# Expanding the split queries of a softmax layer: three transfers of 24 rows for each half

## What is computed

```python
q, k, v = proj(Wq, bq), proj(Wk, bk), proj(Wv, bv)          # 16 heads of 8
scores = einsum('bhqd,bhkd->bhqk', q, k) * scale            # masked (0, 2) or + bias (3)
p = softmax(scores - max(scores))
out = einsum('bhqk,bhkd->bhqd', p, v) @ Wo.T + bo
```

## Time and profile before

| What | us |
|---|---|
| Median of 3 runs | 2870.99 (2866.79 to 2872.88) |
| The profiled execution's own time | 2863.05 |
| Its span in the trace | 2861.2 |
| PE busy in the span | 2431.9 (85%) |
| DVE busy | 1534.3 (54%) |
| ACT busy | 1340.6 (47%) |
| POOL busy | 564.8 (20%) |

### The profile page before, as it was taken

One profiled execution on the slowest core, in us unless ns is written; L12 is line 12 of the kernel. 1 busy time (PEld: TensorE's weight loads), 2 busy tenths in 40 slices (PEclk: granted clock), 3 DMA queues, 4 the chain that ended last, 5 costly groups with the idle time before them and its releaser, 6 DMA issues. The chain is left out here.

```text
span 2861.2 us, 45685 instructions
## 1 busy us (share of the span) xinstructions
PE 2431.9 (85%) x15607; PEld 1470.4 (51%) x15730; DVE 1534.3 (54%) x4364; ACT 1340.6 (47%) x2454; POOL 564.8 (20%) x591
## 2 busy tenths in 40 slices
PE   4688788899994799999996799988886888898887
PEld 2345444588883466666795344444442433444333
DVE  4577667411112366555533566666646776777663
ACT  3355444544443333333134355555551666666665
POOL 1433333000003654553001111111100001111000
PEclk9899999999997799999998699999996999999999
DMA  3222222377773100000264211111102111111011
GB/s 115 75 72 77 77 71 65 105 213 204 207 209 111 29 23 22 23 26 10 80 195 116 71 43 51 51 52 53 57 15 86 46 51 51 51 46 40 33 39 32
DMA packets 132374, 214.08 MB, mean 75 GB/s; under 512 B 22664, under 2 KB 91824, under 8 KB 125232
## 3 DMA queue, kind: packets, MB, share of 16 engines
q1 hardware_dynamic: 119024, 186.88, 22.4%
q0 software_dynamic: 10240, 20.99, 2.6%
q10 hardware_dynamic: 2880, 3.28, 0.4%
HBM read 158.50 MB, written 51.40 MB: 73 GB/s over the span
## 5 line engine op out<-in xcount | busy, mean ns | idle before, releaser
L534 DVE TENSOR_REDUCE arena<-bank 128x1 f32<-128x512 f32 (+4 forms) x1216 | 725.5, 616 | 491.3 <-PE bank L523 258.7
L609 ACT ACTIVATE arena<-bank 128x512 f32<-128x512 f32 x640 | 374.7, 599 | 422.6 <-PE bank L599 349.2
L517 PE MATMUL bank<-arena 125*128 125x512 bf16 (+3 forms) x1536 | 478.5, 348 | 33.5 <-DMA arena<-q_parts 18.4
L587 PE MATMUL bank<-arena 128*128 128x512 bf16 (+3 forms) x1413 | 407.6, 333 | 106.5 <-ACT arena L609 69.7
L609 ACT ACTIVATE arena<-bank,arena 128x512 f32<-128x512 f32 x512 | 337.7, 688 | 213.7 <-PE bank L587 80.9
L587 PEld LDWEIGHTS bank<-arena 128*128 128x128 bf16 x1536 | 139.3, 101 | 413.4 <-ACT arena L609 255.7
L624 PE MATMUL bank<-arena 128*32 128x512 f32 (+3 forms) x3072 | 333.9, 517 | 1.4 <-ACT arena L609 0.8
L938 POOL DMA_INDIRECT back_rows<-sorted_out,back_now x160 | 154.7, 967 | 515.8 <-PE bank L599 231.3
L517 PEld LDWEIGHTS bank<-arena 125*128 125x128 bf16 x1536 | 146.8, 102 | 206.7 <-DVE arena L534 89.0
L1177 ACT ACTIVATE arena<-bank,arena 128x256 f32<-128x256 f32 x320 | 131.9, 471 | 160.0 <-PE bank L1227 160.0
L1022 PE MATMUL bank<-arena 128*128 128x128 f32 x1664 | 202.5, 275 | 0.3 <-ACT arena L1177 0.3
(11 more groups left out here) (250 smaller groups left out, 3558.2 us busy)
## 6 DMA issues: line engine op xcount, KB each, us to landing
arena<-k_parts SPq DMA_DIRECT2D x48, 576.0 KB
arena<-q_parts SPq DMA_DIRECT2D x48, 576.0 KB
arena<-in_L_ffn_w SPq DMA_DIRECT2D x80, 320.0 KB, 3.6
arena<-in_L_ffn_w SPq DMA_DIRECT2D x80, 258.0 KB, 3.1
arena<-sorted_in SPq DMA_DIRECT2D x104, 128.0 KB, 2.5
sorted_out<-arena SPq DMA_DIRECT2D x104, 128.0 KB, 3.5
arena<-in_L_ffn_w SPq DMA_DIRECT2D x24, 512.0 KB, 4.0
k_parts<-arena SPq DMA_DIRECT2D x24, 384.0 KB
```

The source lines that it names most:

```text
L517: ins = pe.matmul(mx[:, k * w:(k + 1) * w], Qx[0:KMAX, h, q * P:(q + 1) * P], Kx[0:KMAX, h, 0:w], start=(k == 0 or not L.causal), stop=not ...
L534: ins = dve.reduce_max(L.mx[:, g % 2, q, heads[0]:heads[-1] + 1], mx[:, 0:w * len(heads) - far].rearrange("p (j k) -> p j k", k=w - far), ...
L587: ins = pe.matmul(st[:, c:c + w], Kx[:, h, kb * P:(kb + 1) * P], Qx[:, h, T - w:T], start=(c == 0), stop=not (L.causal or far), skip_group ...
L609: act.activation(L.probs[:, n % L.PR, 0:w], st[:, 0:w], ACT.Exp, scale=L.scale).then_inc(L.st_free.sem, 1)
```

## The change

Each of the two transfers that fill `Qx` (one for each half of the heads) becomes three, one for each block of 24 rows. They read the same 24 rows of `q_parts` without a repeated dimension. The semaphore of that half counts three completions, and the wait in `pe_max` asks for three. The transfers for `Kx`, the bytes moved and their place in the queue stay: per batch 2 + 6 in place of 2 + 2 transfers.

```diff
-            L.qx = [s(f"q_expanded{i}_", 16, 1) for i in range(HALVES)]
+            L.qx = [s(f"q_expanded{i}_", 16 * NPART, 1) for i in range(HALVES)]
...
-            q_rows = L.qd.rearrange("d i (o h) t -> o (d i) h t", o=1)
+            q_rows = L.qd.rearrange("d i h t -> (d i) h t")
...
-                sp.dma_start(copy_of(L.Qx, b)[0:KROWS, heads, :], q_rows[:, :, heads, :].rearrange(
-                    "o r h t -> o r (h t)").to_broadcast([NPART, NPART * HD, H * T // HALVES])).then_inc(L.qx[half].sem, 16)
+                for j in range(NPART):
+                    sp.dma_start(copy_of(L.Qx, b)[j * NPART * HD:(j + 1) * NPART * HD, heads, :],
+                                 q_rows[:, heads, :]).then_inc(L.qx[half].sem, 16)
...
-                pe.wait_ge(L.qx[half].sem, L.qx[half].at(b, 16))
+                pe.wait_ge(L.qx[half].sem, L.qx[half].at(b, 16 * NPART))
```

## The result

Over 20 runs of each, the changed kernel takes 2884.9 us (2864.8 to 2896.9) and the kernel before 2868.8 (2859.3 to 2876.3): ratio 1.0044, 95% interval 1.0027 to 1.006. The forecast was 2826 us. The profiled execution took 2874.11 us, its span is 2872.3 us against 2861.2, so the two traces hold 11.1 of the 16 us between the medians; the rest lies in executions that weren't profiled.

What follows compares the result with a forecast made beforehand. PE, busy 85% of the span, was taken as the bound, so PE's idle time counts. Gains of 7.5 + 6.5 + 0.3 + 18 + 10 + 3 = 45 us off the 2870.99 us median gave 2826 us, range 2805 to 2857.

Steps and rivals of the forecast that it cites:

- Slower: Rival, chance 0.05: under 160 GB/s, layer 3's max rows stay in line from end to end; 2880 to 2905 us.
- the rate: Expansion transfers: 24 rows spread as `Kx` does go at 209 GB/s, 5.6 us a half, both halves about 12.5 us.
- who holds the row: Layer 3's max row, 6.4 us beside the three-engine tail, would land about 4.6 us after its issue.
- The 3 us for the clock: Layer 3: a shorter stop may spare PE's fall to half clock after the wait; 3 us, between 0 and 8.
- Layer 2's rows: A half is through before the max row is sent, so nearly all 20.0 us of waits go; 18 us less.
- The starts: Starts of layers 0 and 3: `Qx` arrives earlier, 7.5 and 6.5 us less.
- my 5.6 + 2.2: A half's transfer at 209 GB/s plus issue to release when alone: `Qx` 7.8 us after the issue of `Kx`.
- Layer 2's 0.3 us: Start of layer 2: at most 0.3 us less, since its products are in the way.
- Issue: SP's queue: two more issues cost 1.45 us a half, but end no wait of PE; costed at nothing.
- It doesn't spread: Rival, chance 0.06: blocks stay on three engines or run one after the other; +3 us, 2874 us.

Runs made afterwards that it cites:

- e5: Changed kernel, but each half of q is one transfer, 24 rows outermost and three copies inside, parts wrongly paired; ratio 0.9916 to the kernel before.
- e6: Changed kernel, but each block goes to every third partition, parts wrongly paired; ratio 0.9893 to the kernel before.
- e1: Blocks in layers 0 and 2 alone, layer 3 keeps its one transfer; ratio 0.9923 to the kernel before.
- e2: Blocks in layer 3 alone, the old form elsewhere; ratio 1.0085 to the kernel before.
- e4: Kernel before, but layer 3's expansion waits for the third max row of the batch before it, not the second; ratio 0.9939 to the kernel before.
- c4: Kernel before, but in layer 3 the second half of an expansion waits for the third max row; ratio 0.9952 to the kernel before.
- e3: Changed kernel, but layer 3's expansion waits for the third max row of the batch before it, not the second; ratio 0.9842 to the kernel before.
- c3: Changed kernel, but in layer 3 the second half of an expansion waits for the third max row; ratio 0.9802 to the kernel before.
- s1: Changed kernel with a 512-byte transfer behind each block, so that blocks are issued slower; ratio 0.9958 to the kernel before.
- e7: q's parts stored three times in DRAM, each half of q then one plain transfer of 72 rows; ratio 1.0029 to the kernel before.

## Why the prediction was wrong

- **The right mechanism with the wrong sign in layer 3.** That max rows queue with the expansion is what moves this kernel, up and down. The rival *Slower* named what happened, with its place (layer 3's rows in line from end to end) and its condition (under 160 GB/s): its 2880 to 2905 holds the 2884.9. It had a chance of 0.05. Its price was too high in layer 2, which loses nothing, and right in layer 3: 3 to 7 us more in six places, 27 us in all for its 28.
- **The step that failed: the rate.** I took 209 GB/s for a stretch that "holds `Kx` and `Qx` packets together" as what 12 engines give for any transfer. That stretch begins 2 us after the first issue and is mostly `Kx`. The blocks alone had no row before; their rate should have been bounded from below by something else, and the lower bound put into the range. Both halves take 16.8 to 20.1 us for a forecast of 12.5, and no wide form of `Qx` got under 13.9.
- **The second step that failed: who holds the row.** I put layer 3's late row down to the tail on three engines. That is where it was the earlier trace rows, but a wide transfer holds it longer. In e5, which has no tail and 180 GB/s:
```profile
2231.61 0.79 SPq L492 DMA_DIRECT2D arena<-k_parts  x1
...
2238.98 0.72 ACTq L500 DMA_DIRECT2D arena<-arena  x1
...
2247.20 0.61 PE L587 MATMUL bank<-arena 128*128 128x512 bf16 x1 [4.34 <-DMA arena<-arena]
```
  it is in after 8.2 us, for 6.4 with the tail and 11.5 with the blocks. The packets in the traces say why. Alone, the first of a row's 12 packets starts 1.4 us after the issue; here it starts 4.1, 6.4 and 7.5 us after it (before, e5, after). What SP's queue (q1) moved until then, in this order, and below that what both queues moved from there on in before (q10 is ACT's; packets, MB, share of 16 engines):
```profile
q1 hardware_dynamic: 38, 0.29, 19.0%
q1 hardware_dynamic: 162, 1.14, 74.5%
q1 hardware_dynamic: 163, 1.02, 77.4%
...
q1 hardware_dynamic: 14, 0.11, 17.8%
q10 hardware_dynamic: 13, 0.01, 2.1%
```
  That is 77 GB/s on three engines and 179 and 137 on twelve, so a packet of 8 KB takes an engine about 0.32, 0.55 and 0.72 us. The row's first packet is late by 8.5, 9.1 and 8.5 of these: as many go ahead of it on its engine in each form. From there the queues take turns, 13 packets of the row's queue and 14 of SP's in 1.55 us, which costs up to four more for the rest of the row. So a row waits for a number of packets, some 12 in all, and its time is that of a packet: the fewer bytes an engine gets in a microsecond, the later the row. (An estimate; which engine a packet used isn't in the trace.) The step sums say it in time: e5 184.3 and e6 179.0, against 175.6 to 178.4 with the old form. So the 10 us for layer 3's rows weren't to be had at the 180 to 197 GB/s that the best forms reach. The 3 us for the clock went with them: PE stops longer and PEclk is 0.51 for 6 us after.
- **Layer 2's rows: mechanism right.** All its waits are gone, the rows no longer come late, and e1 shows the gain by itself. The two traces differ by 8.6 us there, not 18; over four kernels with each form (before, e2, e4, c4; after, e1, e3, c3) the means are 518.4 and 503.9 us, so the term is 14.5. Part of the scatter is the clock after one of DVE's waits, which both kernels have. Before, with its clock by stretch:
```profile
1851.14 1.12 PE L2006 MATMUL bank<-arena 32*128 32x512 f32 x2 [1.57 <-DVE arena L2044]
...
1853.00:1855.00 2.00, 2.00 (x13) 1.15 (x10) 1.51 (x3) 1.17 (x3) 0.00 (x0) 0.50 0.02 5
1857.00:1859.00 2.00, 2.00 (x22) 1.18 (x14) 1.01 (x2) 0.60 (x1) 0.00 (x0) 1.00 0.48 127
```
and after:
```profile
1975.28 2.07 PE L2007 MATMUL bank<-arena 32*128 32x512 f32 x2 [1.57 <-DVE arena L2045]
...
1975.00:1977.00 2.00, 1.72 (x2) 0.50 (x2) 0.82 (x2) 0.72 (x2) 0.00 (x0) 0.50 0.51 165
1993.00:1995.00 2.00, 2.00 (x13) 0.72 (x15) 1.22 (x2) 0.60 (x1) 0.00 (x0) 0.50 0.74 102
1995.00:1997.00 2.00, 2.00 (x18) 0.76 (x10) 0.69 (x1) 0.75 (x2) 0.00 (x0) 0.93 0.63 107
```
  The same stop of 1.57 us, in different batches of the layer, is followed by 3 to 4 us at 1.2 GHz in the one case and 20 in the other. That the change lengthens it isn't shown: over layer 2's rows the low clock lasts 44 us in before and 58 in after, but 72 in e4 (old form) and 38 in e1 (blocks).
- **The starts: half the size.** 3.8 and 3.5 us for 7.5 and 6.5. Of the 3.4 us that layer 0 missed, the rate is 2: in e5 the first product comes 9.1 us after the first issue (32.8, 41.89), with the blocks 11.2. The other 1.3 are my 5.6 + 2.2, too short even for a fast transfer. Layer 2's 0.3 us can't be told from the scatter.
- **Issue.** The second half's `Kx` is issued 2.24 us after the first one, for 1.6 before, so the two more issues cost 0.6 us in a half and not 1.45, and nothing waits for them. Nothing was right as a price, but slower issue makes these blocks faster (s1).
- **The rule that two transfers to disjoint partitions serialize** (the Trainium skill, page "DMA: Bandwidth & Descriptors", section "Rules for kernel authors"), the ground of the rival *It doesn't spread*, didn't decide here: the blocks did spread, at a share of 0.70 to 0.84.

## What to carry to other kernels

Before a large transfer is spread over more engines, list the small transfers that are sent while it is in flight and who waits for them: on each engine they stand behind packets that now move more slowly, and they gain only if the large one is through before they are sent. If it isn't, order the two: one more entry in a table turned this change from 0.4% slower into 2% faster (each against the old kernel on its own chip). And take a rate from a stretch in which that transfer is alone.

## What the runs showed of the hardware

- The same packets to 24 neighbouring partitions, at the same DMA share of 0.75 to 0.79, move 119 to 139 GB/s, and 188 to 197 when each block is spread over every third of 72 and issued at a slower pace (0.78 us apart for 0.4 to 0.6). A busy share says nothing of bytes.
- Issued 1.1 to 1.2 us apart with a small transfer between them, the neighbouring blocks reach 177 to 185; read from three separate copies at the quick pace, 174 to 194.
- A transfer of 24 rows into neighbouring partitions costs SP 0.366 us to issue, to every third partition 0.704, one of 72 rows 0.727 to 0.764 where its source repeats rows and 0.534 where it doesn't (e7).
- A 12 KB transfer takes 2.2 us alone, up to 5.1 beside one half of blocks and 11.5 beside two, although it is on another queue: by the estimate above 8 to 9 packets of 8 KB go ahead of its first on an engine, then the queues take turns. The Trainium skill, page "DMA: Bandwidth & Descriptors", section "Queues, rings and completion order", says that an engine takes turns between the queues that it has work for, and drains typically 9 to 17 descriptors of one before it switches. The trace agrees with the turns, and with that number for the row's first wait (8.5 to 9.1); after it the turns are of about one packet each (13 and 14 in 1.55 us).
